# Unread products in TensorE's queue: 12 ahead of the first masked product and 48 ahead of tile 4

## The reference

```python
h = maximum(layernorm(x), 0)
H = h @ W_fc + b_fc
scores = (H @ w_att[:d])[:, None] + (H @ w_att[d:])[None, :] + b_att
scores = where(adj > 0, scores, -1e9)        # adj is 4096 x 4096 int32, 64 MB
out = x + softmax(scores, axis=1) @ H
```

## Time and profile before

| | us |
|---|---|
| median of 3 runs | 189.28 |
| lowest and highest | 188.98, 189.49 |
| the profiled execution | 189.04 |
| its span, first to last instruction | 187.3 |
| TensorE (PE) busy in it | 164.5 |
| VectorE (DVE) busy | 144.4 |
| ScalarE (ACT) busy | 32.6 |
| GpSimd (POOL) busy | 7.1 |
| read from HBM | 69.34 MB, 381 GB/s over the span |

### The profile page before, as it was taken

The page is one execution under the profiler, slowest core; times in us unless marked ns, Lnnn a source line. Parts: engine busy times, 40 slices in busy tenths (PEclk is TensorE's granted clock), DMA queues, the critical chain, the costliest instruction groups (busy, mean ns, idle before and its releaser), DMA issues.

```text
span 187.3 us, 2525 instructions
## 1 busy us (share of the span) xinstructions
PE 164.5 (88%) x866; PEld 112.3 (60%) x866; DVE 144.4 (77%) x407; ACT 32.6 (17%) x90; POOL 7.1 (4%) x28
## 2 busy tenths in 40 slices
PE   0449827999999999999999989999999999999950
PEld 0326606666666766666657657577766566776740
DVE  0899869899969887777799996479995644699552
ACT  2346256055068100000040000000000004000010
POOL 2102130000030000000000000000000000000000
PEclk9999995899999999999999999999999999999997
DMA  6999999999999999999999999999999999999202
GB/s 182 385 423 427 422 422 422 420 418 423 418 423 420 420 422 423 422 422 408 419 417 417 417 417 416 420 419 415 414 419 413 420 426 423 416 396 349 81 3 58
DMA packets 13268, 71.61 MB, mean 382 GB/s; under 512 B 1604, under 2 KB 2374, under 8 KB 8134
## 3 DMA queue, kind: packets, MB, share of 16 engines
q1 hardware_dynamic: 12528, 71.18, 92.6%
q10 hardware_dynamic: 726, 0.27, 0.6%
HBM read 69.34 MB, written 2.10 MB: 381 GB/s over the span
## 4 chain that ended last, share of the span: by engine, by line
PE 43%; DMA 22%; DVE 17%; issue 12%; ACT 3%; POOL 2%; DVEq 0%; POOLq 0%
DMA ring<-adj 22%; PE bank L705 16%; PE bank L711 15%; DVE mask L403 8%; PE bank L729 5%; PE bank L753 5%; ACT weighted L325 2%; DVE low L425 2%; DVE mask L412 1%; PE bank L743 1%; DVE stats L419 1%; DVE high_bits L484 1%; DVE x_sb L507 1%; DVE x_sb L515 0%; DVE weighted L592 0%
## 5 line engine op out<-in xcount | busy, mean ns | idle before, releaser
L403 DVE TENSOR_SCALAR mask<-ring 128x2048 fp32r<-128x2048 int32 (+1 forms) x66 | 71.8, 1095 | 24.3 <-DMA ring<-adj 13.8
L705 PE MATMUL bank<-mask,high 128*128 128x512 f32 x256 | 82.1, 424 | 7.9 <-ACT high L331 7.1
L711 PE MATMUL bank<-mask,low 128*128 128x512 f32 x256 | 75.9, 399 | 0.0
L705 PEld LDWEIGHTS bank<-mask,high 128*128 128x128 f32 x256 | 47.3, 197 | 31.2 <-issue 12.6
L711 PEld LDWEIGHTS bank<-mask,low 128*128 128x128 f32 x256 | 49.4, 193 | 11.3
L729 PE MATMUL bank<-mask,w_cols 128*32 128x512 bf16 x256 | 22.8, 393 | 0.9 <-POOL w_cols L305 0.9
L359 ACT COPY sums_T<-bank 128x512 f32<-128x512 f32 x8 | 4.2, 597 | 110.7 <-PE bank L711 110.7
L729 PEld LDWEIGHTS bank<-mask,w_cols 128*32 128x32 bf16 x256 | 4.3, 94 | 13.7 <-issue 12.4
L337 ACT ACTIVATE relu<-x_sb,neg_mean 128x128 f32<-128x128 f32 x32 | 9.7, 394 | 8.8 <-DVEq L439 8.8
L325 ACT ACTIVATE weighted<-relu,w_over_std 128x128 f32<-128x128 f32 x32 | 10.1, 392 | 2.1 <-DVE w_over_std L476 2.1
L515 DVE SCALAR_TENSOR_TENSOR x_sb<-bank,inv_den,x_sb 128x128 f32<-128x128 f32 x32 | 9.0, 344 | 1.7 <-PE bank L753 1.0
(11 more groups left out here) (79 smaller groups left out, 52.0 us busy)
## 6 DMA issues: line engine op xcount, KB each, us to landing
ring<-adj SPq DMA_DIRECT2D x39, 1024.0 KB, 21.2
ring<-adj SPq DMA_DIRECT2D x32, 768.0 KB, 18.0
out<-x_sb SPq DMA_DIRECT2D x7, 256.0 KB, 13.0
x_sb<-x SPq DMA_DIRECT2D x1, 1024.0 KB, 13.6
ring<-adj SPq DMA_DIRECT2D x4, 256.0 KB, 21.9
x_sb<-x SPq DMA_DIRECT2D x1, 768.0 KB, 5.2
x_sb<-x SPq DMA_DIRECT2D x1, 256.0 KB, 3.5
out<-x_sb ACTq DMA_DIRECT2D x2, 64.0 KB, 1.6
```

What stands on the lines that cost most here:

```text
L403: nc.vector.tensor_scalar(mask[:, n % MASKS, 0:cols], ring[:, n % RING, 0:cols], 0.0, None, ALU.is_gt).then_inc(masks_ready, 1)
L705: nc.tensor.matmul(bank[:, b, :], high[:, t, :], mask[:, n % MASKS, cols], start=(t == 0), stop=False)
L711: last = nc.tensor.matmul(bank[:, b, :], low[:, t, :], mask[:, n % MASKS, cols], start=False, stop=(t == T - 1))
```

## The change

Two names are added: `unread`, the identity read as 128x256 numbers of bf16, and `ps_unread`, 256 columns of PSUM bank 7 that are overwritten later. A helper issues a number of products of the first 128 columns of `unread` with all of it; nothing reads their result. TensorE first waits for `constants_ready` (the identity must exist), then does 12 of them, and only then the masked products. 48 more stand ahead of the products of tile 4 in group 0.

```diff
+        ps_unread = bank[:, 7, 0:2 * P]
+        unread = ident[:].bitcast(BF16)
...
             nc.tensor.matmul(ps_lines, ones_row[:], line[:], start=True, stop=True).then_inc(lines_in_psum, 1)
 
+            def keep_working(count):
+
+                for _ in range(count):
+                    nc.tensor.matmul(ps_unread, unread[:, 0:P], unread, start=True, stop=True)
+
+            pe.wait_ge(constants_ready, 1)
+            keep_working(12)
+
             def sums(n):
...
                     if n == LAST:
                         pe.wait_ge(last_masks_ready, i + 1)
+                    if g == 0 and t == STAGES[1][0]:
+                        keep_working(48)
                     if g == 0 and t in [s[0] for s in SPLITS]:
                         pe.wait_ge(high_ready, split_of(t) + 1)
```

## The result

The changed kernel takes 191.25 us (median of 4 runs, 190.25 to 193.4) where the kernel before takes 189.24 (median of 4, 188.98 to 189.49). By the medians that is 2.0 us more. The ratio is 1.0093, 95% interval 1.0072 to 1.0114, or 1.8 us: it leaves out the run of 193.4 us, which is over 1.5% above the shortest and counts as slow. Either way the change is slower by about 1%. The forecast was 192.0 in a range of 190.2 to 194.0. The profiled execution of the change took 190.25 us with a span of 188.3, the shortest of its four; against the profiled execution of before (189.04, span 187.3) that is 1.2 us.

A forecast was written before the change was run, and what follows sets the result against it. Transfers bound the kernel up to 112 us, TensorE after. The fourth pair 4.7 us late, less 1.93 us of slack, leaves 2.8: 189.04 + 2.8 = 191.8 us profiled, median 0.24 above, 192.0 us, range 190.2 to 194.0.

The forecast's parts named there:

- The bound: Transfers of adj set the pace up to 112 us, TensorE from there; TensorE gains before 112 us are worth nothing.
- The slack: TensorE's idle time in four pairs between 84 and 114 us, 1.93 us in sum, absorbs that much lateness.
- The wait for the identity as the dearest part: At TensorE's start: GpSimd makes the identity only at 17.90 after standing still 9.64 us, so TensorE starts 5.5 us later.
- The start: TensorE's first unread product comes at about 17.95, where its masked products started at 12.48 before.
- The 12: The unread products at TensorE's start take 0.22 us each at low clock, 2.6 us together, 17.95 to 20.6.
- The rise of the clock: Full clock comes 5.1 us after steady work starts, 1.7 us either way, so at 23.1.
- The 48: Unread products ahead of tile 4 take 0.12 us each, 5.8 us together, 30.4 to 36.2, nearly all on the path.
- The sum: The fourth pair starts at 40.6, not 35.94, 4.7 us late; 2.8 us are left at 114 us.
- The identity is there in time: Rival, chance 0.08: GpSimd's standstill is 6.9 us or less, the identity exists by 15.1 us, time 189.3 us, not slower.
- The products are dear: Rival, chance 0.05: weight loads aren't hidden, an unread product costs 0.24 us at full clock, time 199.3 us.
- The clock saves: Rival, chance 0.01: removing 2.5 us of low clock at tile 4 makes the kernel faster.

The follow-up runs named there:

- the wait alone: The changed kernel with its wait for the identity but all 60 unread products left out: 189.10 us against 189.15 for the kernel before, ratio 0.9996.
- the wait and the 48: The changed kernel without the 12 unread products at the start: 189.60 us against 189.15 for the kernel before, ratio 1.0035.
- 96 products: The changed kernel with 96 unread products ahead of tile 4 in place of 48: 196.29 us, ratio to the kernel before 1.0376.
- the wait and the 12: The changed kernel without the 48 unread products ahead of tile 4: 189.14 us against 189.15 for the kernel before, ratio 1.0008.
- the early operand: The changed kernel, its 60 unread products reading a tile of ones filled at GpSimd's start, no wait for the identity: 189.19 us against 189.24 before, ratio 0.9993.
- the 48 behind 114 us: The kernel before plus only 48 unread products in group 1, after its 11th pair: 194.36 us against 189.24, ratio 1.0268.

## Why the prediction was right, and where its sizes were off

Point by point, by its own steps.

- **The bound.** Right in what it says of the time and the stretches. Before 112 us a gain is worth nothing (the wait alone: 2.46 us gained and all of it lost), behind 114 us everything counts (48 products: 5.1 us). The reason given was the transfers alone; of the 2.46 us VectorE took 1.73 at 41.66.
- **The slack.** 1.93 us forecast; absorbed were 1.91 in the change, 1.88, 1.90 and 1.97 in three other executions. This was the most useful number of the forecast. It passed over the pair at 40.40, which takes 4.59 us; in the change that pair takes 4.63 without a wait, so it held no slack.
- **The wait for the identity as the dearest part.** Right in that without it the 60 products cost nothing (189.19). Wrong if it is read as a price of its own: the wait alone costs nothing either (189.10). What costs is that the wait uses up the 4.49 us of cover that the 48 then need. The forecast said this of the 48; the runs show it in both directions.
- **The start.** 17.95 forecast, 17.88 measured.
- **The 12.** 2.6 us forecast, 2.39 measured.
- **The rise of the clock.** The step most off. I took 5.1 us from the first product, give or take 1.7. In the change the first four masked products take 1.19 us, which is about 1.4 slow ones and the rest at full pace, so the rise is at 20.9 or a little before, 3.0 us after the first product and outside of my bounds. The 16 masked products took 4.01 us (20.27 to 24.28) where I had 4.8. The two rows behind the 5.1 lay close together (4.9 and 5.35) by chance: with 3.0 in one profile and 5.7 in another, one execution can't say what the middle is.
- **The 48.** 5.8 us forecast, 5.16 measured, and practically all of it on the path, as forecast. The Trainium skill's figure (TensorE: Matmul & The Clock Gate, section Back-to-back issue gap) had given 0.109 us each; the runs give 0.109.
- **The sum.** The start, the 12, the clock and the 48 were 0.07, 0.2, 0.8 and 0.6 us too high. Together they make the fourth pair 2.96 us late where the forecast had 4.7, and after the slack 1.05 where it had 2.8. The median of the runs, though, is 2.0 us above before, nearer to the forecast than the profiled execution, which is the shortest of the four. That nearness is partly luck: four sizes were too high, all on the same side, and what makes up for them in the median is a spread of the executions, which the forecast had only as a bound (the identity 1 us sooner or later).
- **The rivals.** "The identity is there in time" was worked out as 189.3; made real with another operand it gave 189.19. "The products are dear" fell with 0.109 us. "The clock saves" was shown to be void by the wait alone, which gets all of the full clock at tile 4 and no time.

**The spread.** The change's runs lie 3.15 us apart (190.25 to 193.4), those with the wait and the 48 3.0 us, those with 96 products 3.0. The kernel before lies 0.5 us apart in its four runs (0.8 in 25), the wait alone 0.5, the wait and the 12 1.25, the early operand 0.85, and the 48 behind 114 us, without the wait, 0.2. Without the longest run of each the three wide ones are still 1.4, 2.3 and 2.4 us apart. So the wide spread comes with the wait and the 48 together. The clock doesn't explain it: the mean granted clock was 0.985, 0.989 and 0.988 in the longest runs of the three and 0.990, 0.987 and 0.986 in the shortest. The likely cause is that the time of the identity differs between executions (16.86 to 19.53 in ten profiles) and nothing covers it any more. Two things move it: the standstill (8.89 to 10.98 us) and the landing of `a_att` before it. The profile of the wait and the 48 shows one such case, by the second of the two. That the longest runs of the change itself are made so was not seen, since only its shortest was profiled.

## What to carry to other kernels

Before work is added to keep an engine's clock up, find where the chain of waits goes over to that engine: what is saved ahead of that point is lost again at the next wait, and what is added there is paid for only beyond the idle time in between. Sum that idle time from the lengths of like stretches (start to start): here it gave what was absorbed within 0.1 us in the four executions looked at. And look at what a new wait waits for: an operand that is late but needed by nobody in a hurry is a poor choice for work whose operand doesn't matter.

## What the runs showed of the hardware

The standstill of GpSimd ahead of its first `affine_select`, 9.64 us in the chain of before and 9.91 as the timeline counts it there, is by the timeline between 8.89 and 10.98 in nine other profiles, of kernels that do nothing different on GpSimd at that point. The Trainium skill (GPSIMD Engine Reference, section Instruction dispatch) has about 6 us for the load of code at such a first call. No execution here came down to that, and no run shows that the standstill is this load.

The time from TensorE's first product of a stretch to full pace was not constant: about 3.0 us in the change, 3.9 with the wait alone (17.55; one slow product in the four from 21.13), 5.0 with the wait and the 12 and 5.7 with the wait and the 48, the last two by the same count. At tile 4, by the granted clock in four profiles that are alike up to there, the rise came 3.0, 3.6, 5.4 and 5.9 us behind the first product. At the start of a profile the granted clock doesn't show the rise: in the change it is 1.00 from 17.88 to 20.27, where twelve 256-column products took 0.2 us each, about the pace of 1.2 GHz, and in the kernel before it is 1.00 from 12.48 to 17.00, where the first eight products took 3.55 us (12.48 to 16.03), 0.44 each. In these profiles the pace ahead of the first change of clock had to be read from the products. The change first, then the kernel before:

```profile
17.88:20.27 2.39, 2.39 (x12) 1.00 1.00 418
```

```profile
12.48:17.00 4.52, 4.52 (x11) 1.00 1.01 421
```

A product that nobody reads is not free, and costs about what its columns cost: 256 columns in bf16 take 0.108 to 0.109 us at full clock, nearly half of a masked product of 512 columns (0.23). The weight load of each (107 ns on average by the profile of the change) is hidden in that. It is the same at tile 4 (5.16 us for 48) and in a full queue (5.17).
